# Graph layer on one core: the first pair of edge blocks of a round summed ahead of fill 13 and placed behind fill 14

## The reference

```
h = x @ W_node.T + b_node
e = edge_attr @ W_edge.T + b_edge
msg = (h[src] + e) @ W_msg.T + b_msg
s = segment_sum(msg, dst);  deg = number of edges of each target
x = layernorm(x + s / max(deg, 1))      # over the 128 features, eps 1e-5
```

## Time and profile before

| | us |
|---|---|
| median of 3 runs | 718.48 (717.97 to 718.91) |
| the profiled execution's own time | 714.08 |
| its span, first to last instruction | 712.2 |
| PE busy | 647.9 (91%) |
| PE weight loads (PEld) busy | 592.6 (83%) |
| DVE busy | 591.8 (83%) |
| ACT busy | 460.3 (65%) |
| POOL busy | 234.6 (33%) |

### The profile page before, as it was taken

The page is one execution under the profiler, slowest core; times in us unless marked ns, Lnnn a source line. Parts: engine busy times, 40 slices in busy tenths (PEclk is TensorE's granted clock), DMA queues, the critical chain, the costliest instruction groups (busy, mean ns, idle before and its releaser), DMA issues.

```text
span 712.2 us, 22423 instructions
## 1 busy us (share of the span) xinstructions
PE 647.9 (91%) x9313; PEld 592.6 (83%) x9313; DVE 591.8 (83%) x1156; ACT 460.3 (65%) x954; POOL 234.6 (33%) x199
## 2 busy tenths in 40 slices
PE   2699977989999979999999999799999999999994
PEld 2577866878989969999999889798899999989994
DVE  7685697869999868998989899598899898898873
ACT  3147798637657646766767666476677676676772
POOL 3212000210534755434435548354255255000000
PEclk9999999979999999999999999999999999999998
DMA  6881524534556764765865466665755865853400
GB/s 201 288 254 40 168 98 136 186 120 167 185 180 209 254 223 145 263 198 170 279 199 165 153 216 206 213 207 180 233 207 195 260 195 181 274 174 135 143 15 18
DMA packets 81507, 130.55 MB, mean 183 GB/s; under 512 B 12100, under 2 KB 25126, under 8 KB 81303
## 3 DMA queue, kind: packets, MB, share of 16 engines
q1 hardware_dynamic: 73230, 115.79, 48.7%
q0 software_dynamic: 7200, 12.39, 6.2%
q10 hardware_dynamic: 974, 0.90, 0.5%
HBM read 125.80 MB, written 3.23 MB: 181 GB/s over the span
## 4 chain that ended last, share of the span: by engine, by line
PE 75%; DVE 11%; issue 4%; ACT 4%; DMA 3%; POOL 2%; ACTq 0%; DVEq 0%; POOLq 0%
PE x_ps L814 36%; PE count_ps L802 16%; PE win_ps L691 13%; PE win_ps L698 3%; DVE key_hot L954 3%; DVE row_hot L954 2%; PE misc_ps L826 2%; POOL x_gathered L625 1%; DMA x_gathered<-in_x_dram,x_index 1%; PE x_ps L737 1%; DVE x_gathered L1075 1%; PE count_ps L737 1%; ACT counts L1539 1%; DMA win_src<-in_src_dram,clipped_int 1%; PE x_ps L721 1%
## 5 line engine op out<-in xcount | busy, mean ns | idle before, releaser
L814 PE MATMUL x_ps<-x_parts,counts 128*125 128x256 f32 x2254 | 391.2, 301 | 6.5 <-ACT counts L1544 6.5
L1547 ACT CAST counts<-count_ps 128x490 fp32r<-128x490 f32 x552 | 321.9, 604 | 105.3 <-PE count_ps L802 102.5
L814 PEld LDWEIGHTS x_ps<-x_parts,counts 128*125 128x125 f32 x2254 | 299.6, 189 | 9.8 <-ACT counts L1544 9.8
L625 POOL DMA_INDIRECT x_gathered<-in_x_dram,x_index x144 | 186.6, 1296 | 243.8 <-PE count_ps L802 231.0
L954 DVE TENSOR_TENSOR row_hot<-iota_bf,row 125x3200 bf16<-125x3200 bf16 x115 | 209.6, 1822 | 50.9 <-PE count_ps L802 29.3
L802 PE MATMUL count_ps<-key_hot,row_hot 125*128 125x98 bf16 x2875 | 216.5, 209 | 12.8 <-ACT counts L1547 9.4
L802 PEld LDWEIGHTS count_ps<-key_hot,row_hot 125*128 125x128 bf16 x2875 | 149.2, 98 | 44.1 <-issue 11.3
L954 DVE TENSOR_TENSOR key_hot<-iota_bf,key 125x2500 bf16<-125x2500 bf16 x115 | 167.2, 1454 | 0.0
L691 PE MATMUL win_ps<-edges,onehot 128*32 128x128 f32 x3232 | 104.6, 282 | 0.2 <-DVE sums_e L944 0.2
L691 PEld LDWEIGHTS win_ps<-edges,onehot 128*32 128x32 f32 x3232 | 88.1, 113 | 9.1 <-issue 1.4
L1448 ACT COPY win_sb<-win_ps 128x128 f32<-128x128 f32 x110 | 29.0, 267 | 72.5 <-PE win_ps L691 70.8
(11 more groups left out here) (214 smaller groups left out, 417.2 us busy)
## 6 DMA issues: line engine op xcount, KB each, us to landing
edges<-in_edge_attr_dram SPq DMA_DIRECT2D x101, 1024.0 KB, 6.8
resid<-in_x_dram SPq DMA_DIRECT2D x25, 125.0 KB
out_dram<-y SPq DMA_DIRECT2D x25, 125.0 KB
x_gathered<-in_x_dram,x_index POOLq DMA_INDIRECT x144
region<-in_dst_dram ACTq DMA_DIRECT2D x1, 768.0 KB
win_src<-in_src_dram,clipped_int POOLq DMA_INDIRECT x23, 3.6
x_index<-in_src_dram SPq DMA_DIRECT2D x9, 8.0 KB, 5.8
region<-in_L_gnn_W_node_dram SPq DMA_DIRECT2D x1, 64.0 KB
```

The source lines that it names most:

```text
L625: pool.indirect_dma_start(out=x_gathered[:, i, :], out_offset=None, in_=x[:, :], in_offset=bass.IndirectOffsetOnAxis(ap=x_index[:, k, i:i ...
L814: mm = pe.matmul(x_ps[m % 2][0:PB, h * 2 * D:(h + 1) * 2 * D], counts[h][:, b, :], x_parts[:, b, :, :].rearrange("p k d -> p (k d)"), star ...
L1547: ins = act.copy(counts[h][:, :, at - h * PB:at - h * PB + FILL * 2], nodes)
```

## The change

On all three engines that follow the items' order, a slot's items are bound to a fill. `sum_at(s)` is 3 for slot 2 and 0 for the others: PE sums, and ACT copies, ahead of fill `sum_at(s)` of the slot, and PE places behind the fill after it. For slots 0, 1, 3 and 4 that is the old position. For slot 2 the sums go from ahead of fill 10 to ahead of fill 13, the copies from ahead of the move of fill 10 to ahead of that of fill 13, and the places from behind fill 11 to behind fill 14 and the piece of `apply_counts` that follows it. DVE's and SP's lists are unchanged; they meet the items when PE is done with them.

```diff
+        def sum_at(s):
+            return 3 if s == 2 else 0
...
             for u in range(SLOTS):
                 g = u - LEAD
-                for v in items_at[u]:
-                    sum_windows(v)
                 if u < LEAD:
                     t = blocks_at[u][0]
+                    sum_windows(u)
...
                 for f in range(FILLS):
+                    for v in items_at[u] if f == sum_at(s) else []:
+                        sum_windows(v)
                     count_fill(g, f)
...
-                    for v in items_at[u] if f == 1 else []:
+                    for v in items_at[u] if f == sum_at(s) + 1 else []:
                         place_windows(v)
...
-                for v in items_at[u]:
-                    copy_windows(v)
+                if u < LEAD:
+                    copy_windows(u)
...
                 for f in range(FILLS):
+                    for v in items_at[u] if f == sum_at(s) else []:
+                        copy_windows(v)
                     move_bank(g * FILLS + f)
```

## The result

The kernel took 722.6 us (median; 721.3 to 724.8), the kernel before 718.55 on the same chip: a ratio of 1.0058, with an interval of 1.0040 to 1.0076. So 4.05 us were lost, where 2.2 were predicted. The profiled execution of after took 721.58 (span 719.7, mean granted clock 0.965), that of before 714.08 (712.2, 0.979). The clock makes part of that difference: between the first fill and 700 us, about 24 us are at the lower level before, and 44 after.

The account below looks back on a forecast made before the run. PE was taken to bound the kernel, so its idle gaps count. 3.4 us gained and 5.6 lost, net 2.2 lost on 718.48, gave 720.7 us; its own range 719.5 to 722, and 716.8 to 723 leaving out the ends.

Parts of the forecast that it names:

- three signs: Wrong if rounds 1 and 2 together under 2 us longer, slot 3's sums don't wait, or PE waits for edge data.
- rounds 6 and 13: Sum of gathered rows waits 3.9 us for the last gather, issued behind POOL's own queue: 0 change.
- The wait that goes: Ordinary rounds: ACT moves fill 12 beneath the sums, so PE's 0.46 us stall behind fill 14 goes; 7 rounds, 3.2 gained.
- Gathered rounds: Rounds 5, 8, 10, 12, 17, 19: slot 3's sum waits 0.61 us for the add, against 0.46 gained; 0.15 lost each.
- Round 3: DVE's add comes 0.96 us later, so slot 4's one-hots are late and fill 20 waits for them: 0.6 us lost.
- Round 1: ACT's moves delay copies, places and DVE's add; the chain to PE's 3.05 us wait has no slack: 2.1 us lost.
- second rival: Not slower: ACT's start in round 1 and `make_degrees` in round 2 hang on something besides the adds; 717.2 us, chance 0.17.
- third rival: As forecast, but the clock stays low longer around the two lengthened waits: 721.7 to 723.1 us, chance 0.20.
- Round 2: Add comes at 142.05 instead of 140.66; keys, one-hots and `make_degrees` behind it delay PE's 3.07 us wait: 1.4 us lost.
- Queues passed: SP's loads of blocks t+3 and t+4 come 1.9 us later; of 3.2 us slack 1.3 remain: 0 cost, cover thin.
- Clock: Low stretches around the waits in rounds 1 and 2 taken as they are; if longer, up to 2.4 us more together.
- Edge data late: A pair's second load comes after its sum in six gathered rounds, up to 1 us each: 721.7 to 726.7, chance 0.13.

Follow-up runs that it names:

- the first four kernels: Pair moved only in some rounds, against the kernel before (716.22): 0 to 3, 721.94 us; 6 and 13, 721.18; plain, 713.43; gathered, 716.46.

## Why the prediction was right or wrong

The direction was right and the size was half of what came: 4.05 us, in a range that went to +4.5. None of the three signs that the prediction named for being wrong came. That the time lies inside the range is in part luck, for a term that was put at 0 (rounds 6 and 13) cost 3.6 to 5.0 us when it was moved alone, and the range was not made for it.

**The wait that goes**: right. -0.49 in each of seven plain rounds for -0.46, and the moved plain rounds by themselves gave -2.8 us.

**Gathered rounds**: the wait for the add exists, but in five of the six it is 0.35 to 0.38 us on PE, where the wait for fill 12 was 0.31 on PE; the one is traded for the other, and the rounds come out at -0.03 to -0.07 and not at +0.15. (which the 0.45 us from a place to its add come from, is of round 7 and not 8; nothing hangs on it.) Round 5 has 0.62 on PE and comes out at +0.57, but not because it is moved: it takes 27.8 us too in the kernels where its order is the old one and round 4 is 27.2 to 27.4 us long, and 27.22 where it is moved and round 4 takes 28.56. Part of what round 4 gains when it has no low clock is lost again in round 5.

**Round 0**: +0.41 for 0.6. **Round 3**: +0.55 for 0.6, by fill 20's wait for one-hots, 0.33 us.

**Round 1**: the chain was right and exposed, so the second rival falls. ACT ends its passes 0.93 later within the round, and the add comes 3.07 later: behind ACT it is the predicted 2.14. That it agrees so well is luck: ACT's copies come 1.47 behind the passes, for the 1.9 predicted, and the add 1.54 behind the copies, for 1.1, since the clock is low while PE places (four matmuls in 1.16 us from 113.43, for the 0.65 of the earlier trace rows). The 0.93 are from slot 0, where the clock is at 0.50 after and was at 1.00 before (97 to 103 us, windows above), behind a wait of 2.69 us that the change does not touch. Four of the kernels with the old order in rounds 0 and 1 (6 and 13 moved, plain rounds moved, gathered rounds moved, later loads) show a low stretch there too and take 37.6 to 37.7 us for round 1 instead of 36.76, so these 0.93 are not the change's. The fill follows by +3.11. PE's own wait for it grew only from 3.05 to 3.56, for about 5 predicted, because PE stands 1.35 us at fill 13 already and is slower in between. The clock behind it takes 0.8 more (0.50 against 0.89 from 121 to 127): the third rival, in part.

**Round 2**: the add is 1.25 later and PE's transpose 1.24, for 1.4. Only 0.65 are left at the round's end. The low clock, which began inside the wait, covers 9.2 us behind it before (147.31 to 156.5) and 7.9 after (153.21 to 161.1). The longer wait lies in a stretch that was slow already, and gives about half of these 1.3 us back.

**Rounds 6 and 13**: this is the step that failed, a term put at 0. "That gather is issued by POOL behind its own queue, not paced by the fills moved here: what is gained before is waited for there, 0." The first half holds: the gather is issued at 14.11 and 14.12. PE waits not for its issue but for its packets, and these come through behind the pair's edge loads, whose issue moves by 1.9 us with the sums. That 1.9 stands in the prediction, under "Queues passed", but was weighed only against the edge blocks' own due times. The two rounds are 2.51 and 2.29 us longer by the profiles; of the first an unknown part is chance, as said above. Loads put later without the change cost 4.7 us, and held back gained 7.5.

**Clock**: the stretches were taken as they are. By the profiles they went up in rounds 1, 6 and 13 (3.4 us of low clock behind each gather wait became 6.8) and down in round 4 (-1.25, a stretch that is gone). In round 11, where nothing is moved, a wait of 1.35 us is the same in both kernels, and only after it is followed by low clock, which costs 1.56.

**Edge data late** (fourth rival): did not come; no wait of PE for an edge block appears among the waits of the kernel after. The loads were late for another transfer.

So, by the two profiles: 3.8 us lost by the chains of the first four rounds (0.41 + 2.14 + 0.65 + 0.55, for 4.7 predicted), 4.8 in rounds 6 and 13; 3.8 gained (7 x 0.49, and 0.4 in rounds 8, 10, 12, 15, 16, 17 and 19); and the clock takes 1.8 in round 1 and 1.6 in round 11 and gives 0.7 in rounds 4 and 5 together. That makes 7.5. The forecast of 2.2 lacked the gathers' 4.8 and had the chains 0.9 too high. Of these 7.5 us, 0.9 in round 1 and perhaps 2 in round 6 come in the old order too, in some profiles and not in others. They would account for most of what the profiles differ beyond the 4.05, but the executions without a trace can't be looked at for it.

How much of the loss is clock is not settled either. As an estimate from the two traces: between the first fill and 700 us PE is busy for 22.0 us at the lower level before and for 35.0 after. If all of that work took twice as long as at the upper level, the 13.0 more would have cost 6.5 of the 7.5 us; that is an upper bound. The parts above that are called chains and gathers hold some of it, for low stretches lie behind the waits that grew. The six executions of after had a mean granted clock of 0.963 to 0.970, the 27 of before beside the first four kernels 0.973 to 0.984. No run here changes the order and holds the clock, so the rival that the clock carries much of the loss stands. Behind the waits for the gathers, which grew, the low stretches grew too; in rounds 4 and 11 they went and came with waits that grew by 0.28 us or not at all.

## What to carry to other kernels

A load that is moved is to be checked against every transfer that shares the DMA engines with it, above all small late ones on which an engine waits, and not only against the due time of its own data. Before a step is put later to fill a repeated small stall, list what stands behind its last consumer in each engine's order and move the urgent part ahead; here the stall was worth 3.8 us in all, and by the profiles the chains and the gathers behind it cost 8.6. Where the order and such a mend are both to be had, try the mend alone first: holding two loads back gained 7.5 us, twice what the order could give.

## What the runs showed of the hardware

A small gather of POOL whose packets run beside a megabyte load of SP starts them 2.7 to 3.7 us after its issue, and one without such a load beside it 0.7 us after (round 6 of the kernel after; the last gather is issued by 263.49 and starts at 267.19, behind the gather before it). Held until the last gather had landed, the second load of two pairs gave back 7.5 us.

The granted clock fell behind waits much shorter than those of 3 us. The same wait of 1.35 us, in round 11, leaves it at 1.00 before (393 to 397) and at 0.57 after (400 to 404). Over the profiled runs it was low in the kernels with rounds 7 and 9 moved (25.4 us for the round) and not in the others (23.9), so it repeats with the order of the rounds before it; what decides it is open. In slot 0 of round 1, behind one and the same wait of 2.69 us, kernels that do the same until then show no low stretch or one of 3.4 or 6.8 us.
